# Attention's half batches reordered, and an SBUF copy and a VectorE eviction moved

## The reference, cut to what matters

```python
q, k, v = (qkv[:, :, 0], qkv[:, :, 1], qkv[:, :, 2])
scale = D ** (-0.5)
scores = jnp.einsum('blhd,bmhd->bhlm', q * scale, k)
attn = jax.nn.softmax(scores, axis=-1)
o = jnp.einsum('bhlm,bmhd->blhd', attn, v).reshape(b, l, c)
```

## Time and profile before

| what | value |
| --- | --- |
| median of 3 runs | 3257.01 us (3256.4 to 3257.45) |
| profiled execution, its time | 3255.73 us |
| profiled execution, its span | 3254.0 us |
| attention's half batches, start of first to last reduction | 409.4 to 2154.5 us |

### The profile page before, as it was taken

How to read it: one execution, slowest core, us unless ns; L and a number is a source line. 1 busy time by engine, 2 the same in 40 slices (tenths; PEclk the granted TensorE clock), 3 DMA queues, 4 the chain that set the end, 5 groups by cost and what they waited for, 6 DMA issues and landing times. The chain is left out here.

```text
span 3254.0 us, 52481 instructions
## 1 busy us (share of the span) xinstructions
PE 3238.2 (100%) x19049; PEld 2117.3 (65%) x19049; DVE 2161.4 (66%) x4134; ACT 1695.6 (52%) x3183; POOL 358.3 (11%) x284
## 2 busy tenths in 40 slices
PE   9999999999999999999999999999999999999999
PEld 7888744444444444444444444449998898989988
DVE  6444488888888888888888888857633433433332
ACT  4323377777777777777777777765611112211110
POOL 0000010111100000010000000026411010000000
PEclk9999999999999999999999999999999999999999
DMA  7554442333323232323232333328722122421211
GB/s 241 179 165 149 153 93 59 75 74 76 66 59 66 59 65 56 68 63 69 59 69 59 65 63 65 63 63 276 238 95 77 53 82 71 142 69 57 80 46 55
DMA packets 187841, 299.53 MB, mean 92 GB/s; under 512 B 66783, under 2 KB 87791, under 8 KB 180670
## 3 DMA queue, kind: packets, MB, share of 16 engines
q1 hardware_dynamic: 187582, 296.17, 34.1%
HBM read 193.99 MB, written 101.43 MB: 91 GB/s over the span
## 5 line engine op out<-in xcount | busy, mean ns | idle before, releaser
L1306 DVE TENSOR_REDUCE q_mx<-b_st 128x1 f32<-128x512 f32 x1512 | 988.6, 681 | 147.8 <-PE b_st L1240 142.8
L1380 ACT ACTIVATE b_pt<-b_st 128x512 f32<-128x512 f32 x2048 | 1055.1, 609 | 8.6 <-PE b_st L1256 8.5
L1268 PE MATMUL b_op<-b_pt,b_vs 128*37 128x512 f32 x4096 | 981.5, 600 | 2.1 <-DVE b_ob L1349 2.1
L1373 ACT ACTIVATE b_early<-b_st 128x512 f32<-128x512 f32 x504 | 302.3, 600 | 451.3 <-PE b_st L1240 451.3
L1268 PEld LDWEIGHTS b_op<-b_pt,b_vs 128*37 128x37 f32 x4096 | 203.5, 113 | 444.3 <-issue 360.2
L2125 PE MATMUL d_pm<-d_vh,d_ah 128*128 128x288 f32 x1152 | 339.3, 295 | 0.8 <-DVE d_al L2163 0.8
L2126 PE MATMUL d_pm<-d_vl,d_ah 128*128 128x288 f32 x1152 | 339.5, 295 | 0.0
L2127 PE MATMUL d_pm<-d_vh,d_al 128*128 128x288 f32 x1152 | 339.5, 295 | 0.0
L1306 DVE TENSOR_REDUCE q_mx<-b_early 128x1 f32<-128x512 f32 x504 | 339.4, 673 | 0.0
L1444 POOL TENSOR_TENSOR w_oc<-b_oa,b_ob 37x512 f32<-37x512 f32 x127 | 161.3, 1270 | 1440.4 <-DVE b_ob L1349 1437.4
L1240 PEld LDWEIGHTS b_st<-q_hh,b_qa 36*128 36x128 f32 x1024 | 128.7, 184 | 223.5 <-DVE q_mx L1306 197.7
(11 more groups left out here) (414 smaller groups left out, 4685.7 us busy)
## 6 DMA issues: line engine op xcount, KB each, us to landing
qkh<-a_th SPq DMA_DIRECT2D x72, 256.0 KB, 2.1
qkl<-a_tl SPq DMA_DIRECT2D x72, 256.0 KB, 2.3
d_yi<-y SPq DMA_DIRECT2D x64, 288.0 KB, 3.0
n_oi<-hw SPq DMA_DIRECT2D x12, 1024.0 KB, 5.8
vd<-a_vx SPq DMA_DIRECT2D x8, 1184.0 KB, 6.6
b_vs<-vd SPq DMA_DIRECT2D x32, 296.0 KB, 3.0
a_x<-in_x SPq DMA_DIRECT2D x8, 1152.0 KB, 6.8
q_qs<-qkh SPq DMA_DIRECT2D x32, 288.0 KB
```

The source lines that it names most:

```text
L1268: ins = e.matmul(op[64 * a:64 * a + VW, :], vs[h % 2][:, j + 8 * a, :], pt[g % NP][:, a * 512:a * 512 + 512], start=j == 0, stop=j == 7)
L1306: e.tensor_reduce(mx[:, k // 2, col:col + 1], src, AX.X, ALU.max).then_inc(s_mx, 1)
L1373: e.activation(early[:, :], bank(slot)[:, :], ACT.Copy).then_inc(s_cp, 1)
L1380: e.activation(pt[g % NP][:, a * 512:a * 512 + 512], bank(k)[:, :], ACT.Exp, scale=SCALE).then_inc(s_p, 1)
```

## The change

In each half batch the order on TensorE and in the plan of uses becomes scores, scores, maxima, maxima. The copy to `early` is gone, and VectorE reduces all four banks of maxima in PSUM, in their order. The tile's SBUF space stays reserved under the name `gap`. Of a finished block, ScalarE evicts the half at partition 64 to `oa`, at the start of a half batch ahead of its exponentials, and VectorE the other half to `ob`. ScalarE's half has a semaphore of its own, `s_od`, and all who waited for two counts of `s_oa` now wait for one of each.

```diff
@@ LastBlock
-        e.activation(self.oa[:, :], self.op[64:64 + VW, :], ACT.Copy).then_inc(self.s_oa, 1)
+        e.activation(self.oa[:, :], self.op[64:64 + VW, :], ACT.Copy).then_inc(self.s_od, 1)
...
-        e.wait_ge(self.s_oa, 2 * self.n)
+        e.wait_ge(self.s_oa, self.n)
+        e.wait_ge(self.s_od, self.n)
@@ phase_attention
-    early = A.sb("early", [128, 512])
+    A.sb("gap", [128, 512])
...
-        for kind in ("mx", "st", "st", "mx"):
+        for kind in ("st", "st", "mx", "mx"):
...
             if kind == "st":
                 e.wait_ge(s_p, n + 1)
-            elif kind == "mx" and n % 4 == 0:
-                e.wait_ge(s_cp, n // 4 + 1)
             elif kind == "mx":
-                e.wait_ge(s_mx, n if n % 4 == 1 else n + 1)
+                e.wait_ge(s_mx, n + 1)
...
             elif j == 0:
-                e.wait_ge(s_oa, 2 * blk)
+                e.wait_ge(s_oa, blk)
+                e.wait_ge(s_od, blk)
...
         for s in plan:
-            for u in s.units[0:1]:
-                score_max(*u)
             for x in s.scores:
                 scores_t(*x)
-            for u in s.units[1:2]:
+            for u in s.units:
                 score_max(*u)
...
-            for a in (0, 1) if c else (1, 0):
-                src = bank(slots[a])[:, :]
-                if c or a:
-                    e.wait_ge(s_s, m + a + 1)
-                else:
-                    e.wait_ge(s_cp, m // 4 + 1)
-                    src = early[:, :]
+            for a in range(2):
+                e.wait_ge(s_s, m + a + 1)
                 col = 2 * c + a
-                e.tensor_reduce(mx[:, k // 2, col:col + 1], src, AX.X, ALU.max).then_inc(s_mx, 1)
+                e.tensor_reduce(mx[:, k // 2, col:col + 1], bank(slots[a])[:, :], AX.X, ALU.max).then_inc(s_mx, 1)
...
-                e.tensor_copy(oa[i][:, :], op[64:64 + VW, :]).then_inc(s_oa, 1)
                 e.tensor_copy(ob[i][:, :], op[0:VW, :]).then_inc(s_oa, 1)
...
-        def first_out(n, slot, _):
-
-            m = 2 * (n - THERE)
-            e.wait_ge(s_s, m + 1)
-            if m:
-                e.wait_ge(s_mx, m - 2)
-            e.activation(early[:, :], bank(slot)[:, :], ACT.Copy).then_inc(s_cp, 1)
+        def block_out(n):
+
+            e.wait_ge(s_pv, 8 * (n + 1))
+            if n > 1:
+                e.wait_ge(s_oc, n - 1)
+            e.activation(oa[n % 2][:, :], op[64:64 + VW, :], ACT.Copy).then_inc(s_od, 1)
...
-            for u in s.units[0:1]:
-                first_out(*u)
+            if s.block is not None:
+                block_out(s.block)
...
-                e.wait_ge(s_oa, 2 * s.block + 2)
+                e.wait_ge(s_oa, s.block + 1)
+                e.wait_ge(s_od, s.block + 1)
```

More of the change, by code:

```diff
@@ L231, with __init__ @@
 class LastBlock:
-    def __init__(self, op, oa, ob, oc, s_pv, s_oa, s_oc, s_o):
+    def __init__(self, op, oa, ob, oc, s_pv, s_oa, s_od, s_oc, s_o):
         self.op, self.oa, self.ob, self.oc = op, oa, ob, oc
-        self.s_pv, self.s_oa, self.s_oc, self.s_o = s_pv, s_oa, s_oc, s_o
+        self.s_pv, self.s_oa, self.s_od, self.s_oc, self.s_o = s_pv, s_oa, s_od, s_oc, s_o
         self.n = NH * 4
@@ L1071, in phase_attention @@
     s_s, s_mx, s_nm, s_mt, s_mh = A.sem("s"), A.sem("mx"), A.sem("nm"), A.sem("mt"), A.sem("mh")
-    s_cp, s_md = A.sem("cp"), A.sem("md")
+    s_od, s_md = A.sem("od"), A.sem("md")
     s_st, s_p, s_pv, s_oa, s_oc = A.sem("st"), A.sem("p"), A.sem("pv"), A.sem("oa"), A.sem("oc")
@@ L1464, in phase_attention @@
         block.gpsimd(gpsimd)
-    return LastBlock(op, oa[1], ob[1], oc[1], s_pv, s_oa, s_oc, s_o[1])
+    return LastBlock(op, oa[1], ob[1], oc[1], s_pv, s_oa, s_od, s_oc, s_o[1])
 def phase_proj(nc, A, W, rest, first, N, ident, ks0, adaT, eps, gd, xf, ot, sm, W_fc1, b_fc1, hth, htl, hw,
```

## The result

The changed kernel takes 3371.07 us (median of 4 runs, 3370.62 to 3374.53) against 3257.23 us before (4 runs). The ratio is 1.0353, with a 95% interval of 1.0337 to 1.0368. It is slower by 114 us; 118 were forecast, in a range that holds the result. The profiled execution took 3374.53 us, its span is 3372.8 us; it is the longest of the four.

The account below looks back on a forecast made before the run. TensorE was taken as the bound, busy 3238.2 of 3254.0 us. Products' loads move from T+1.61 to T+1.84 (T: a half batch's first weight load); 502 x 0.235 = 118 us more gives 3375 against the median, range 3345 to 3402.

Parts of the forecast that it names:

- The forecast's step: TensorE's last pair of maxima: its second bank waits for the first exponential instead of the copy, 0.235 us per half batch.
- The sum: Products' load after a half batch's first weight load (T): exponential's start, its duration, release, remaining distance; T+1.84 against T+1.61.
- 504 x 0.60 come off ScalarE: Copies to SBUF gone from ScalarE, no bound: gain at most 0.02 us per half batch, if the bank were free early.
- the rival that the copy's wait is won: Exponential frees the bank in time; only the 0.02 offset in the pair comes back: 10 us, 3247; chance 0.03.
- the 0.11 behind the 63 us: Part of the held weight load's delay that could lie beside the pair's other matmul, making the cost 63 us.
- The forecast's cover: VectorE's reductions, first at about T+1.6, end 0.37 into the next half batch; banks needed at T+1.05: cover 0.6 us.
- never the reverse: Sign in the changed trace: VectorE's reductions should wait for TensorE, and TensorE never for reductions.
- my cover of 0.16: ScalarE's output eviction from T+0.12 lets the exponential start at T+0.61, before T+0.77: cover 0.16 us, no cost.
- The rival that the clock falls: TensorE's clock drops to its lower level; one half batch in ten low adds 120 us, 3495; chance 0.03.

## Why the prediction was right

- **The bank's reader.** The forecast's step, that the eighth use now waits for the first exponential and that this alone sets the half batch, is shown by moving the release both ways: +0.53 and -0.22 us of it moved the time by +264 and -107 us, and 502 x 0.53 = 266, 502 x 0.22 = 110. Taking the eighth use away brings both kernels within 0.1% of each other.
- **The sum.** Its terms read 0.77, 0.60, 0.05 and 0.42, T+1.84; the trace has 0.77, 0.60, 0.05 and 0.43, T+1.85. The half batch grew by 0.23 where I took 0.235. Taking the exponential's start from the last half batches, which had no maxima, was right: the same T+0.77.
- **The whole.** 118 were forecast, 114 measured by medians. The two profiled executions are 118.8 apart, but only 115.9 of that lie where the forecast put all of it; the rest is start and end. That 118 and 118.8 agree so closely is partly luck. Some 4 us lie between one execution and the other, and what they are stays open.
- **Small terms.** "504 x 0.60 come off ScalarE" is too much for its busy time: 171 us came off, with 127 evictions new on it. Busy time counts overlapping instructions once, and a copy with an exponential 0.49 behind it adds 0.49; 504 x 0.49 - 127 x 0.60 = 171. It changed nothing in the sum. No row shows the 0.02 of the rival that the copy's wait is won, nor the 0.11 behind the 63 us; the half batch of 3.44 without the eighth use, against 3.46, fits the 0.02.
- **Reductions and row maxima.** VectorE's first reduction starts at T+1.54, not 1.6, and waits for TensorE, also behind the row maxima (0.24 of idle time). The forecast's cover held, but "never the reverse" has one exception, in the half batch that VectorE's one reciprocal of 3.33 us (L175) makes late. It takes 4.55 us instead of 3.69; the one in the kernel before takes 4.32 instead of 3.46, so it isn't part of the difference:

```profile
PEld b_st L1239 <- DVE q_mx L1299: 1.1, 3, 0.4
```

The run with only the order changed shows how thin the cover is for the eviction: with both halves and a later copy it fails.

- **The eviction.** Free in the changed kernel, as forecast (T+0.11 to the exponential at 1509.91, T+0.77), but my cover of 0.16 was too large. It rested on a spacing of 0.49 that a copy and an exponential have; this eviction keeps 0.62, so 0.04 are left. In the changed kernel's timeline, from T = 1509.14:

```profile
1509.25 0.59 ACT L1364 ACTIVATE b_oa<-b_op 37x512 f32<-37x512 f32 x1 [0.98 <-PE b_op L1268]
...
1509.91 2.06 ACT L1371 ACTIVATE b_pt<-b_st 128x512 f32<-128x512 f32 x4
```

- **The weight load that waits.** The held load came 0.05 after the exponential's end in the changed kernel, and 0.04 after the copy's end (1509.15) in the run with only the eviction moved. So the rule of the Trainium skill ("TensorE: Matmul & The Clock Gate", The mechanism) on weight loads pulled ahead of matmuls in flight, by which it would have been 63 us, gave nothing back for a load that carries the wait.
- **The clock** stayed at 1.00 (2.4 GHz), with a pause in each half batch; also where it was three times as long, in the run with the swapped exponentials:

```profile
430.00:2400.00 1970.00, 1842.99 (x9349) 763.54 (x9347) 1331.01 (x2454) 1040.18 (x1998) 177.78 (x138) 1.00 0.25 53
```

The Trainium skill's case of a clock that swings while cycling through PSUM banks ("TensorE: Matmul & The Clock Gate", A second HAM failure mode) didn't show in these. The clock did fall once in each of two other runs, behind the reciprocal: without the copy in the old order, where TensorE had stood idle for 1.67 us in one piece, and in the changed kernel with seven uses. Such a half batch took 6.45 and 6.65 us, once in the whole run, 2 or 3 us of each time. In the first of them:

```profile
1455.11 0.50 PE L1239 MATMUL b_st<-q_ks,q_qs 36*128 36x512 f32 x1 [1.67 <-DVE q_mx L1301]
...
1456.00:1458.00 2.00, 2.00 (x8) 0.27 (x4) 0.85 (x2) 0.00 (x0) 0.00 (x0) 0.62 0.00 0
1458.00:1460.00 2.00, 2.00 (x10) 1.44 (x10) 0.87 (x2) 0.08 (x1) 0.00 (x0) 0.53 0.00 0
```

The rival that the clock falls was thus a real one, but not for a pause of 0.23 or 0.76 in each half batch.

## What to carry to other kernels

With n banks used in turn and n + 1 uses in a period, one use waits for a reader in its own period. Count which one it is, and give that bank the reader that can start soonest and end soonest; a copy that looks like waste on the busy-share page can be the quickest release there is. Before removing it, compute the release of whatever takes its place, from the timeline and against the slot of the waiting instruction, and try a half-sized reader, which leaves out part of the work but shows at once how much of the time hangs on that release.

## What the runs showed of the hardware that I had not expected

- A ScalarE eviction of 37 x 512 from partition 64 of PSUM to partition 0 of SBUF keeps 0.62 us to the ScalarE instruction before it and to the one behind it. From partition 0 to partition 0, the next one follows after 0.50, as between a copy and an exponential. In 126 half batches this was 3280.44 against 3262.81 us. That the shift of partitions is the cause is shown for this pair of halves only.
- After TensorE had stood idle for 1.67 us once, in a stretch in which it was otherwise busy, the granted clock was 0.62 and 0.53 in the next two stretches of 2 us, and 1.00 again behind them (the run without the copy in the old order).
- An exponential over 256 columns took 384 ns where one over 512 takes 602 on the mean: half the columns are worth 0.22 of 0.60 us.
